# Windowed attention of two layers: weighted values per query with a column of ones for the sums, division on the way out of PSUM, result transposed on TensorE

## What is computed

```python
# per layer; 8 heads of 64, windows of 64 tokens
qkv = shift_token(x) @ wqkv
q, k = l2norm(q) * qs, l2norm(k) * ksc          # then rotary with xpos
bk, bv = look_around(bk), look_around(bv)        # own window and the one before: 128 keys
sim = einsum('bhwid,bhwjd->bhwij', bq, bk)       # masked outside i-64 .. i
attn = softmax(sim, axis=-1)
out = einsum('bhwij,bhwjd->bhwid', attn, bv)
x = x + o @ wo
h = layernorm(shift_token(x)) * lg + lb
a, g = split(h @ w1 + b1)
x = x + (a * gelu(g)) @ w2 + b2
```

## Time and profile before

| | us |
|---|---|
| median of the runs | 1438.56 (1438.05 to 1438.8) |
| the profiled execution | 1443.03 |
| its span | 1441.2 |

### The profile page before, as it was taken

The page is one execution under the profiler, slowest core; times in us unless marked ns, Lnnn a source line. Parts: engine busy times, 40 slices in busy tenths (PEclk is TensorE's granted clock), DMA queues, the critical chain, the costliest instruction groups (busy, mean ns, idle before and its releaser), DMA issues.

```text
span 1441.2 us, 35736 instructions
## 1 busy us (share of the span) xinstructions
PE 1266.9 (88%) x12288; PEld 987.5 (69%) x12288; DVE 1294.1 (90%) x2514; ACT 872.1 (61%) x1468; POOL 951.0 (66%) x753
## 2 busy tenths in 40 slices
PE   5889899989989889988788999999999889999986
PEld 3577677767767767766566777777777767777764
DVE  4899999999999999997798988999899898999975
ACT  3556566565666656554456676676676657666661
POOL 0733443344433444346799899999999999999973
PEclk8899999999999999998899999999999999999998
DMA  5000000000000000000111112111111121212111
GB/s 170 1 10 13 12 5 11 11 11 11 9 11 11 11 7 5 8 9 14 36 44 41 41 41 49 38 39 42 45 45 48 41 50 43 51 40 49 45 30 31
DMA packets 87332, 44.24 MB, mean 31 GB/s; under 512 B 43938, under 2 KB 80460, under 8 KB 87244
## 3 DMA queue, kind: packets, MB, share of 16 engines
q1 hardware_dynamic: 87244, 43.08, 12.0%
HBM read 19.99 MB, written 6.29 MB: 18 GB/s over the span
## 4 chain that ended last, share of the span: by engine, by line
DVE 39%; issue 23%; POOL 19%; PE 15%; SPq 2%; DVEq 1%; ACT 1%; POOLq 1%; DMA 0%; ACTq 0%
DVE sums L973 9%; DVE probs L1005 7%; POOL rnorm L654 5%; DVE mx L999 4%; POOL kT L646 4%; POOL kT L662 4%; POOL probs L720 4%; PE bank L1372 3%; DVE xo L1034 2%; PE bank L1359 2%; PE bank L1454 2%; PE bank L1427 2%; DVE hc L1077 2%; SPq L475 1%; DVE conv L916 1%
## 5 line engine op out<-in xcount | busy, mean ns | idle before, releaser
L622 POOL TENSOR_TENSOR probs<-probs,coef 128x1024 f32<-128x1024 f32 x128 | 239.5, 1901 | 202.3 <-DVE coef L965 202.3
L795 ACT ACTIVATE probs<-probs 128x1024 f32<-128x1024 f32 x128 | 134.8, 1053 | 100.5 <-DVE probs L1005 100.0
L654 POOL TENSOR_TENSOR rnorm<-norm,halves 128x16 f32<-128x16 f32 x64 | 187.4, 2928 | 3.3
L1274 PE MATMUL bank<-ident,probs 128*128 128x128 f32 x1024 | 143.4, 285 | 49.6 <-POOL probs L622 49.6
L999 DVE TENSOR_REDUCE mx<-bank 128x8 f32<-128x512 f32 x256 | 163.8, 681 | 16.5 <-PE bank L1287 15.2
L782 ACT ACTIVATE wT<-bank 128x512 f32<-128x512 f32 x256 | 138.9, 596 | 65.4 <-PE bank L1274 64.4
L646 POOL TENSOR_TENSOR kT<-qT 128x512 f32<-128x512 f32 x128 | 162.9, 1273 | 22.5 <-DVE qT L1053 20.0
L1005 DVE TENSOR_TENSOR probs<-bank,mx 128x512 f32<-128x512 f32 x256 | 163.6, 680 | 0.0
L1274 PEld LDWEIGHTS bank<-ident,probs 128*128 128x128 f32 x1024 | 115.9, 145 | 68.6 <-POOL probs L622 57.5
L1287 PE MATMUL bank<-kT,qT 64*128 64x256 f32 x1024 | 155.7, 425 | 5.4 <-DVE probs L1005 5.4
L811 ACT ACTIVATE qT<-bank 128x512 f32<-128x512 f32 x128 | 75.9, 593 | 134.0 <-PE bank L1354 126.4
(11 more groups left out here) (118 smaller groups left out, 3074.2 us busy)
## 6 DMA issues: line engine op xcount, KB each, us to landing
probs<-f_v SPq DMA_DIRECT2D x96, 128.0 KB, 2.3
res<-stage_x SPq DMA_DIRECT2D x48, 128.0 KB, 3.7
xn<-in_x SPq DMA_DIRECT2D x16, 128.0 KB, 2.2
xr<-in_x SPq DMA_DIRECT2D x16, 128.0 KB, 2.1
stage_x<-xo SPq DMA_DIRECT2D x32, 64.0 KB, 1.6
hn<-stage_x SPq DMA_DIRECT2D x32, 64.0 KB
mn<-mid SPq DMA_DIRECT2D x64, 32.0 KB
stage_x<-yo SPq DMA_DIRECT2D x16, 128.0 KB, 2.1
```

What stands on the lines that cost most here:

```text
L622: nc.gpsimd.tensor_tensor(out=e[:, :, :, :], in0=e[:, :, :, :], in1=coef[r][:, 2, A_REP * ng:A_REP * (ng + 1), :].unsqueeze(3).broadcast_t ...
L654: nc.gpsimd.tensor_tensor(out=rnorm[:, at], in0=norm2[:, 1, at], in1=halves[:, 0:2 * F_HEADS], op=ALU.pow).then_inc(rnorm_set, 1)
L1274: ins = nc.tensor.transpose(banks[4 + hp][:, P * (2 * kb + hh):P * (2 * kb + hh + 1)], e[:, 2 * hh + hp, 2 * kb:2 * kb + 2, :], ident[:, :])
```

## The change

The kernel no longer divides the attention weights. The values get a column of ones (`F_VW` = 65 columns a head), so the product of weights and values gives the sum of the weights as its 65th column. The operands of that product are exchanged: the transposed weights are loaded and the values are streamed, and the result lies as (query, head dimension) in banks 4 and 5. DVE divides on the way out (`heads_scaled`), PE transposes the result with four transposes (`heads_transposed`) behind the projection of v, and ACT copies it to `foT` behind the copy of v. The sums on DVE and the product on POOL are gone. Both sets of `qkT` now stand together behind the weighted values (in tile 1 behind `values` too), in banks 0 and 1. The guard of the squared norms moves from DVE to POOL, ahead of the power. The ring of exponentials has two places in place of four.

```diff
-F_RING = 4
+F_RING = 2
+F_VW = F_HD + 1
@@
             if kind == "qkT":
-                return banks[5]
+                return banks[local % 2]
@@ POOL, inverse_norms
+                    pool.wait_ge(norm_step, 4 * unit + 2 * tile + 2)
+                    nc.gpsimd.tensor_scalar_max(norm2[:, 1, at], norm2[:, 0, at], NORM_FLOOR).then_inc(guarded, 1)
                     pool.wait_ge(guarded, TILES * unit + tile + 1)
@@ POOL, body
-                        if f_exists(turn, s):
-                            e = fE[s % F_RING]
-                            pool.wait_ge(f_rsum_set, n + 1)
-                            nc.gpsimd.tensor_tensor(out=e, in0=e, in1=f_rsum[s % 2][:, :, :].unsqueeze(3).broadcast_to([P, 2, 4, F_KEYS]),
-                                                    op=ALU.mult).then_inc(f_normed, 1)
@@ ACT, body
                         if prepares(turn, p, tile):
-                            transposed(unit + tile, 4 * (p + tile) + 2 - 2 * tile, 2 - 2 * tile, turn)
-                        if f_exists(turn, s, F_ATT_LAG):
-                            act.wait_ge(f_o_made, late + 1)
...
-                        if prepares(turn, p, tile):
-                            transposed(unit + tile, 4 * (p + tile) + 3 - 2 * tile, 3 - 2 * tile, turn)
+                            for m in (2 - 2 * tile, 3 - 2 * tile):
+                                transposed(unit + tile, 4 * (p + tile) + m, m, turn)
                         if prepares(turn, p):
                             values_read(unit + 1, TILES * (p + 1) + tile, tile, turn)
+                        if f_exists(turn, s, F_ATT_LAG):
+                            act.wait_ge(oT_made, late + 1)
+                            wait(act, f_made["out"], late - 1)
+                            nc.scalar.activation(foT[(s - F_ATT_LAG) % 2][:, :, :], banks[4].rearrange("p (m q) -> p m q", m=INNER // P),
+                                                 ACT.Copy).then_inc(f_o_read, 1)
@@ DVE
-                def guard(index, unit, tile):
...
-                def exponentials_summed(n, s):
-
-                    dve.wait_ge(f_exp, n + 1)
-                    nc.vector.tensor_reduce(f_sum[s % 2][:, :, :], fE[s % F_RING], AX.X, ALU.add).then_inc(f_sum_set, 1)
...
+                def heads_scaled(late, r):
+
+                    dve.wait_ge(f_o_made, late + 1)
+                    out = heads_out[:, :, 0:4 * F_VW].rearrange("p b (h d) -> p b h d", h=4)
+                    nc.vector.reciprocal(f_rsum[r][:, :, :].unsqueeze(3), out[:, :, :, F_HD:F_VW]).then_inc(f_rsum_set, 1)
+                    dve.wait_ge(f_rsum_set, late + 1)
+                    wait(dve, oT_made, late - 1)
+                    nc.vector.tensor_tensor(fo[r].rearrange("p (b h d) -> p b h d", b=2, h=4), out[:, :, :, 0:F_HD],
+                                            f_rsum[r][:, :, :].unsqueeze(3).broadcast_to([P, 2, 4, F_HD]), ALU.mult).then_inc(fo_set, 1)
@@ PE
-                    pe.wait_ge(f_normed, late + 1)
+                    pe.wait_ge(f_exp, late + 1)
                     wait(pe, f_o_read, late)
-                    if unit is not None:
-                        wait(pe, f_read["qkT"], 4 * unit + 2 * tile + 2)
+                    wait(pe, fo_set, late)
@@ PE, weighted_values
-                    for m in range(4):
+                    for h in range(F_HEADS):
                         for w in range(2):
-                            for hh in range(2):
-                                h = 2 * m + hh
-                                ins = nc.tensor.matmul(banks[4][F_HD * hh:F_HD * (hh + 1), P * m + WINDOW * w:P * m + WINDOW * (w + 1)],
-                                                       (f_v if w else f_vs)[p][:, tile, h, :], eT[:, h, WINDOW * w:WINDOW * (w + 1)],
-                                                       start=True, stop=True)
+                            ins = nc.tensor.matmul(banks[4 + h // 4][WINDOW * w:WINDOW * (w + 1), F_VW * (h % 4):F_VW * (h % 4 + 1)],
+                                                   eT[:, h, WINDOW * w:WINDOW * (w + 1)], (f_v if w else f_vs)[p][:, tile, h, :],
+                                                   start=True, stop=True)
                     ins.then_inc(f_o_made, 1)
+
+                def heads_transposed(late, r):
+
+                    pe.wait_ge(fo_set, late + 1)
+                    for m in range(INNER // P):
+                        ins = nc.tensor.transpose(banks[4][:, P * m:P * (m + 1)], fo[r][:, P * m:P * (m + 1)], ident[:, :])
+                    ins.then_inc(oT_made, 1)
@@ PE, body
-                        if prepares(turn, p, tile):
-                            if follows:
-                                pe.wait_ge(eT_read, 2 * late + 2)
-                            ahead("qkT", 4 * (p + tile) + 2 - 2 * tile)
                         if follows:
                             weighted_values(it, late, late_s // TILES, late_s % TILES)
                         following("values")
                         if prepares(turn, p, tile):
-                            pe.wait_ge(f_read["qkT"], 4 * (unit + tile) + 3 - 2 * tile)
-                            ahead("qkT", 4 * (p + tile) + 3 - 2 * tile)
+                            pe.wait_ge(f_sub, n + 1)
+                            for m in (2 - 2 * tile, 3 - 2 * tile):
+                                ahead("qkT", 4 * (p + tile) + m)
                         if prepares(turn, p):
                             ahead("v", TILES * (p + 1) + tile)
+                        if follows:
+                            heads_transposed(late, late_s % 2)
```

More of the change, by code:

```diff
@@ L178, in sem @@
             return ctx.enter_context(nc.semaphore(name))
-        banks = [ctx.enter_context(nc.psum_tensor(f"bank{i}", [P, 512], FP32)) for i in range(8)]
+        heads_out = ctx.enter_context(nc.psum_tensor("heads_out", [P, 2, 512], FP32))
+        banks = [heads_out[:, i - 4, :] if i in (4, 5) else ctx.enter_context(nc.psum_tensor(f"bank{i}", [P, 512], FP32)) for i in range(8)]
         x_in = t["x"].rearrange("b (t p) d -> p b t d", p=P)
@@ L324, in build @@
             sem(n) for n in ("squared", "norm_step", "guarded", "added", "rnorm_set", "qk_normed"))
-        f_scored, f_max, f_sub, f_exp, f_sum_set, f_rsum_set, f_normed, eT_made, eT_read = (
-            sem(n) for n in ("f_scored", "f_max", "f_sub", "f_exp", "f_sum_set", "f_rsum_set", "f_normed", "eT_made", "eT_read"))
+        f_scored, f_max, f_sub, f_exp, f_rsum_set, fo_set, oT_made, eT_made, eT_read = (
+            sem(n) for n in ("f_scored", "f_max", "f_sub", "f_exp", "f_rsum_set", "fo_set", "oT_made", "eT_made", "eT_read"))
         vs_in = [sem(f"vs{p}_in") for p in range(PAIR)]
@@ L1039, in layers_program, with rotate @@
             def layers_program():
-                def rotate(index, local, m, turn, layer):
+                def rotate(index, before, local, m, turn, layer):
                     tile, kind = divmod(m, 2)
@@ L1054, in rotate @@
                                             tab(1).rearrange("p h (t d) -> p h t d", t=2), ALU.mult).then_inc(rotated, 1)
+                    wait(dve, guarded, TILES * before + tile + 1)
                     nc.vector.tensor_reduce(norm2[:, 0, F_HEADS * m:F_HEADS * (m + 1)],
                                             sq[m % 2][:, :].rearrange("p (h d) -> p h d", h=F_HEADS), AX.X, ALU.add).then_inc(norm_step, 1)
-                def guard(index, unit, tile):
-                    dve.wait_ge(norm_step, index + 1)
-                    wait(dve, rnorm_set, TILES * (unit - 1) + tile + 1)
-                    at = slice(2 * F_HEADS * tile, 2 * F_HEADS * (tile + 1))
-                    nc.vector.tensor_scalar_max(norm2[:, 1, at], norm2[:, 0, at], 1e-24).then_inc(guarded, 1)
                 def stats(x, st, out, bn, done, count):
@@ L1155, in beside @@
                             m = fill[1]
[L1156 to L1158 removed]
+                            rotate(m, -1, m, m, "pre", 0)
                     a_body(TURNS, "drain", beside)
[L1162 to L1168 removed]
+                def heads_scaled(late, r):
[6 more added lines that the diff above has]
+                                            f_rsum[r][:, :, :].unsqueeze(3).broadcast_to([P, 2, 4, F_HD]), ALU.mult).then_inc(fo_set, 1)
                 def body(it, turn, layer_of):
@@ L1213, in body @@
                             at = 2 * tile + 1
-                            rotate(4 * (unit + 1) + at, 4 * (p + 1) + at, at, turn, layer_of(p + 1))
-                            guard(4 * (unit + 1) + at, unit + 1, tile)
+                            rotate(4 * (unit + 1) + at, unit, 4 * (p + 1) + at, at, turn, layer_of(p + 1))
                         if late("z") is not None and layer_of(late("z")) == LAYERS - 1:
@@ L1430, in scores, with weights_transposed @@
                     ins.then_inc(f_scored, 1)
-                def weights_transposed(late, r, unit, tile):
-                    pe.wait_ge(f_normed, late + 1)
+                def weights_transposed(late, r):
```

(6 more changed lines are left out.)

34 lines of the change are left out of this document (15 added, 19 removed).

## The result

| | before | after |
|---|---|---|
| median of four runs, us | 1438.68 (1438.05 to 1440.41) | 1463.97 (1463.00 to 1465.94) |
| ratio, 95% interval | | 1.0174 (1.0161 to 1.0187) |
| profiled execution, its span, us | 1443.0, 1441.2 | 1464.5, 1462.5 |
| mean granted clock over the span | 0.971 | 0.968 |

What follows compares the result with a forecast made beforehand. No busy share named the bound; in tile 1 PE's value matmuls wait for DVE's `mid`. 17 x 0.88 + 12 x 1.24 = 30 more gave 1473 profiled, 1468.6 as a median (1468 at 1455 to 1477, 45%); range 1437 to 1485.

Steps and rivals of the forecast that it cites:

- V: Start of tile 1's value matmuls after its scores, set by DVE's `mid`: 7.82 in layer 0, 8.07 in layer 1.
- L662 no longer stalls PE, only the idle time ahead of V grows, to some 1.7: Tile 1: PE stops waiting for POOL's inverse-norm products, but idles some 1.7 before the value matmuls.
- L662 starts 3.65 after the scores, over L1077: Layer 0, tile 1: POOL's products start 0.65 ahead of DVE's `hc` pair and overlap it; the pair ends at 5.78.
- The rule of thumb: Where POOL's products start ahead of DVE's `hc` pair, the pair was taken to end 0.08 after the second product.
- DVE's new pair 0.83: Each step on DVE: reciprocal of 8 columns and product of 512 out of PSUM, 0.83 (0.75 to 1.2).
- The weighted values 0: Sixteen weighted-value products on PE with 65 columns and exchanged operands: no change from 1.08, loss of up to 1.08 possible.
- Rival (d): Exchanged operands with 65 columns break the overlap of pairs on PE: 1.08 more a step, total 1492; 8%.
- The heads' transposes +0.41, not waiting in layer 0 and waiting till 8.35 in layer 1: Four added PE transposes behind the projection of v: 0.41 a step; layer 1's tile 0 waits for DVE's new pair.
- Tile 0's step 10.30: Layer 0, tile 0, scores to next scores: 4.16 + 0.80 + 4.52 + 0.82 = 10.30, against 10.40 before.
- Filling and draining 0 (-2 to +3): Kernel's start and end: shorter path to the values and longer one behind about cancel, 0 (-2 to +3).
- The steady steps, 17 x 0.88 + 12 x 1.24 = 30: 17 units of layer 0's pattern lose 0.88 each, 12 with layer 1's work 1.24 each: 30 in total.
- The clock, 2%: Transposes not counting as array activity and longer idle bring PE to 1.2 GHz, 1.8 a unit or more: 1520; 2%.

Runs made afterwards that it cites:

- a: Changed kernel with tile 1's eight q/k transposes put ahead of the MLP's value matmuls, not behind them; 1437.03 us, ratio 0.9983.
- b: Changed kernel with one wait added: in tile 1 POOL starts its products with the inverse norms only after DVE has written `hc`; 1427.92 us, ratio 0.9910.
- i: Changed kernel with work added: in tile 0 DVE also sums the exponentials, result unused, so POOL gets its input later; 1434.31 us, ratio 0.9962.
- g: Changed kernel with the heads' four transposes done twice in both steps; 1475.43 us, ratio 1.0250.
- h: Changed kernel with the guard of the squared norms moved from POOL back to DVE; 1455.39 us, ratio 1.0109.
- e: Kernel before with DVE writing `mid` ahead of `hc` and the rotation in tile 1, one more SP wait; 1452.10 us, ratio 1.0090.
- f: Kernel before with `mid` ahead of `hc` in tile 1 and POOL's products held until `hc` is written; 1446.97 us, ratio 1.0059.

## Why the prediction was right, and where it wasn't

The mechanism is the forecast one, and V and the steps came out close. That the total did so too is in good part luck (last paragraph).

| | forecast | measured |
|---|---|---|
| tile 0, layer 0 | 10.30 | 10.48 |
| V, layer 0 | 7.82 | 7.66 to 7.84 |
| V to the scores | 4.98 | 4.85 |
| tile 1, layer 0 | 12.80 | 12.49 to 12.70 |
| unit, layer 0 | 23.10 (+0.88) | 22.95 to 23.16 (+0.84 on average) |
| V, layer 1 | 8.07 | 8.14 to 8.28 |
| tile 0 and 1, layer 1 | 11.19, 13.05 | 11.09, 13.00 and 13.13 |
| unit, layer 1 | 24.24 (+1.24) | 24.09 to 24.22 (+1.10 to 1.24) |

*L662 no longer stalls PE, only the idle time ahead of V grows, to some 1.7.* Right: no idle time before L1355 in layer 0, and 1.75 before the values. a shows the converse.

*L662 starts 3.65 after the scores, over L1077.* Right: 919.63 - 915.97 = 3.66, and `hc` takes 1.50 (forecast 1.48). But two misses cancel in the 3.66: counted from the scores before, the products start at 14.14 and not 13.95, mostly for the maximum, and tile 0's step is 0.18 longer than forecast. And this is the later of two patterns in layer 0: over its 15 units the start is 3.42 to 3.67, the pair 1.31 to 1.50. In layer 1, with the scores at 1246.94, it starts 4.07 after (forecast 3.9), the pair takes 1.94, and V is 8.28 (rows of DVE and of PE, below). b and i show that this is what V hangs on. The rule of thumb, that the pair ends 0.08 behind the second product, holds only if a tensor_scalar gets in between the products; in g it ends 0.34 behind, in 11 of h's units too. The maximum took 0.25, with waits 0.41 up to the power's start, against 0.28.

```profile
1251.24 1.94 DVE L1074 TENSOR_SCALAR hc<-mn,mmv,mrstd 128x128 f32<-128x128 f32 x2
```
```profile
1255.22 1.13 PE L1368 MATMUL bank<-hT,w 128*128 128x256 f32 x4 [2.19 <-DVE mid L1143]
```

*DVE's new pair 0.83.* 911.83 to 912.67, 0.84. The stepped read of two banks costs no more than L1053 does.

*The weighted values 0.* 910.55 to 911.63, 1.08, as in the earlier trace rows. Rival (d) is out.

*The heads' transposes +0.41, not waiting in layer 0 and waiting till 8.35 in layer 1.* 0.43; no wait in layer 0, and in layer 1 one of 0.29:

```profile
1268.42 0.66 PE L1456 MATMUL heads_out<-ident,probs 128*128 128x128 f32 x4 [0.29 <-DVE probs L1164]
```

That is 8.35 after the scores at 1260.07.

*Tile 0's step 10.30.* Too low by 0.18. The second projection, with what follows it to the weighted values, takes 0.89 (909.66 to 910.55) and not 0.80. The eight transposes take 0.85 and the heads' four 0.43, 0.05 more than the 0.82 and 0.41 that I counted; the last 0.04 is spread over the step. The copy to `foT` costs nothing, as forecast, though it lets ACT's gelus begin 0.13 later behind the gates' matmuls than before.

*Filling and draining 0 (-2 to +3).* This term was mis-sized: the filling's eight steps took 7.2 less. The waits of PE over the filling show why, those for POOL's products before (from 695 to 755) and after (693 to 750):

```profile
PE bank L1359 <- POOL kT L662: 6.1, 4, 1.7
```
```profile
PE bank L1355 <- POOL kT L671: 0.3, 1, 0.3
```

In the filling the MLP does not run yet, so no value matmuls wait for `mid`, and the end of POOL's stall is worth what it promises. The case for the change held just there, for eight steps of 63; I had dismissed it by weighing the paths of one unit, and not read the stretch's own waits. Behind the last scores the order of the kernel makes no difference that the traces show: 42.3 in e and f, 41.8 to 42.2 in a, b and g.

*The steady steps, 17 x 0.88 + 12 x 1.24 = 30.* Too high by 9. Measured were 12.6 in layer 0's pattern and, without the drops of the clock, 14.7 - 6.4 = 8.3 behind it. 15 units and not 17 stand outside the filling (2.4 of the 9). Ten units with layer 1's work, and not 12, took 11.7 more in all, 1.17 each (3.2). The two others, at the change-over between the layers, took 0.7 less, and the very last step 2.7 less (11.95 before, 9.28 after), of which some 1.3 is the drop that the kernel before has there. My units described neither.

*The clock, 2%.* The rule as priced (every unit, 52 us) did not come, but a part of it did: 6.4 in four steps and 3.1 behind the last scores. The prediction had nothing between none and all.

*The total.* In the two profiles the steps and the filling make 12.6 + 8.3 - 7.2 = 13.7, where the forecast had 30. The clock's 9.5, and 1.9 of scatter the other way, make it the 21.3 between the spans, and the medians lie 25.3 apart. So the forecast of 29.4 owes its closeness to misses of opposite sign: by its own terms alone the changed kernel would have come out some 15 us slower, with the kernel before's drop taken out too. That estimate is from one traced execution of each kernel.

## What to carry to other kernels

Find out what the engine that sets the end waits for last, and on which side of that wait an edit puts work: ahead of it the work is free as far as the idle time reaches, behind it every tenth counts, and relieving engines that don't produce the thing waited for only makes them wait longer. Where a POOL product and a pair of DVE's tensor_scalars can meet, their order within hundredths of a microsecond is a term of the sum of its own, so an instruction that becomes faster or moves must be followed to the next such meeting. And a change that loses may have moved the bound to where one cheap edit takes it off: this one with two edits that cost 7 us on the kernel before gives 1402.80, 2.65% faster than it.

## What the runs showed of the hardware

- One instruction of 1.2 us more on DVE in each unit made the kernel 30 us faster (i against the changed kernel), by keeping POOL's products off `hc`; some 6 of the 30 are steps at the low clock that i doesn't have.
- Two fp32 tensor_scalars of 128x128 take 0.60 alone, 1.32 when they start 0.18 ahead of POOL's two products of 128x512, 2.10 when they start 0.02 behind, 1.94 at 0.23 behind, 1.50 at 0.63 and 1.45 at 0.93. The two products take 2.04 to 2.16 in all these cases.
- Of the changed kernel's idle times ahead of the value matmuls (27 in the stretch, 1.8 us on average), three let the clock down, each for part of one step; g and h show no drop in the steady stretch.
- The sixteen fp32 products of the weighted values take 1.08 us with 65 columns as with 64, and with the operands exchanged.
